# Expert outputs added by the scatter into four sums per token, in place of six rows

## What is computed

```
x = x + attn0(layernorm(x));  x = x + ffn0(layernorm(x))      # per-token attention; 2 experts, top 1
x = x + ssm(layernorm(x));    x = x + moe(layernorm(x))       # state space scan; 64 experts, top 6
def moe(h):                                                   # 2048 tokens, E = 64, TOP_K = 6, CAP = 64
    scores = softmax(h @ gate_w.T);  w, expert = top_k(scores, 6)
    for e in range(64):            # the first 64 (CAP) tokens that chose e, in token order; later ones are dropped
        out[e] = (silu(buf[e] @ w_gate[e]) * (buf[e] @ w_up[e])) @ w_down[e]
    y[t] = sum over the 6 choices of w[t, k] * out[expert[t, k]][slot of t]
    return y + shared expert(h)
```

## Time and profile before

| What | us |
|---|---|
| time, median of 3 runs | 720.53 |
| time of the profiled execution | 720.47 |
| its span in the profile | 718.7 |
| up to the first gather of an expert pair | 0 to 564.6 |
| pair stage, to the landing of the last scatter | 564.6 to 675.8 |
| loads, sums and stores of the result | 675.8 to 718.7 |

### The profile page before, as it was taken

One profiled execution on the slowest core, in us unless ns is written; L12 is line 12 of the kernel. 1 busy time (PEld: TensorE's weight loads), 2 busy tenths in 40 slices (PEclk: granted clock), 3 DMA queues, 4 the chain that ended last, 5 costly groups with the idle time before them and its releaser, 6 DMA issues.

```text
span 718.7 us, 7161 instructions
## 1 busy us (share of the span) xinstructions
PE 591.0 (82%) x2225; PEld 329.1 (46%) x2225; DVE 511.9 (71%) x1100; ACT 198.9 (28%) x387; POOL 105.6 (15%) x119
## 2 busy tenths in 40 slices
PE   4348999789999589988879997959658499999874
PEld 3234665436555445553444653543245144444553
DVE  4995878066986759998599996879965545555364
ACT  1111321225442064341633324412201133332100
POOL 3020221300002000002000020000000446664200
PEclk9766999998999699999998998979977699999999
DMA  8921000409101067011650023868071269998497
GB/s 312 382 86 45 29 31 9 124 31 351 67 29 36 1 236 249 1 37 29 236 212 1 1 66 119 293 229 289 0 241 38 64 242 371 363 358 299 148 412 295
DMA packets 50371, 114.35 MB, mean 159 GB/s; under 512 B 6112, under 2 KB 32992, under 8 KB 49824
## 3 DMA queue, kind: packets, MB, share of 16 engines
q1 hardware_dynamic: 42576, 94.88, 37.1%
q0 software_dynamic: 5456, 16.91, 6.9%
q10 hardware_dynamic: 2304, 2.10, 0.8%
HBM read 84.26 MB, written 29.62 MB: 158 GB/s over the span
## 4 chain that ended last, share of the span: by engine, by line
PE 52%; DVE 25%; DMA 6%; ACT 4%; issue 3%; SPq 2%; POOL 1%; DVEq 0%; POOLq 0%; ACTq 0%
PE gate_ps L675 7%; PE up_ps L675 7%; PE gate_ps L806 6%; PE misc_ps L692 6%; DVE scan_area L1219 6%; PE ssm_ps L725 4%; PE turn_ps L626 4%; DMA bc<-part_rows 3%; DVE scan_area L1215 3%; PE misc_ps L777 3%; PE ssm_ps L824 3%; DVE scan_area L1222 3%; PE misc_ps L824 2%; DVE sig L1159 2%; PE turn_ps L797 2%
## 5 line engine op out<-in xcount | busy, mean ns | idle before, releaser
L675 PE MATMUL gate_ps<-big,front_area 128*128 x160 | 81.1, 632 | 1.9 <-ACT front_area L864 1.9
L692 PE MATMUL misc_ps<-big,front_area 128*128 x320 | 75.1, 389 | 2.6 <-ACT front_area L864 1.6
L1219 DVE TENSOR_TENSOR_SCAN scan_area<-scan_area 128x1024 f32<-128x1024 f32 x32 | 73.3, 2292 | 5.5 <-ACT scan_area L964 2.0
L675 PE MATMUL up_ps<-big,front_area 128*128 x160 | 75.2, 592 | 0.0
L692 PEld LDWEIGHTS misc_ps<-big,front_area 128*128 128x128 f32 x320 | 62.0, 195 | 21.0 <-issue 13.1
L725 PE MATMUL ssm_ps<-scan_area,ident 128*128 128x512 f32 x128 | 62.8, 627 | 4.7 <-DVE scan_area L1222 4.2
L900 ACT ACTIVATE sig<-gate_ps 128x512 f32<-128x512 f32 (+1 forms) x52 | 30.9, 595 | 126.0 <-PE up_ps L675 90.0
L1159 DVE SCALAR_TENSOR_TENSOR sig<-sig,gate_ps 128x512 f32<-128x512 f32 (+1 forms) x52 | 35.5, 683 | 25.2 <-ACT sig L900 24.8
L964 ACT ACTIVATE scan_area<-scan_area,a_col 128x511 f32<-128x511 f32 x64 | 41.9, 713 | 32.0 <-DVE scan_area L1219 30.8
L584 POOL DMA_INDIRECT front_area<-ysorted_dram,slot_idx x16 | 18.0, 1126 | 220.6 <-DMA ysorted_dram<-front_area 217.0
L675 PEld LDWEIGHTS up_ps<-big,front_area 128*128 128x128 f32 x160 | 30.8, 192 | 39.6 <-issue 39.6
(11 more groups left out here) (213 smaller groups left out, 886.8 us busy)
## 6 DMA issues: line engine op xcount, KB each, us to landing
bc<-bc_dram SPq DMA_DIRECT2D x4, 4096.0 KB, 13.3
part_rows<-zeros SPq DMA_DIRECT2D x16, 768.0 KB, 16.4
big<-in_wgu SPq DMA_DIRECT2D x15, 704.0 KB
front_area<-in_wgu SPq DMA_DIRECT2D x9, 704.0 KB
big<-part_rows SPq DMA_DIRECT2D x8, 768.0 KB, 10.1
scan_area<-in_wgu SPq DMA_DIRECT2D x6, 704.0 KB
big<-in_wd SPq DMA_DIRECT2D x15, 256.0 KB
front_area<-part_rows SPq DMA_DIRECT2D x5, 768.0 KB, 20.7
```

The source lines that it names most:

```text
L675: mm = pe.matmul(bank[:], xs_t[:, k, j, :], gu0[:, expert_of[b, j], k, g, half * 512:(half + 1) * 512], start=(k == 0), stop=(k == K - 1))
L692: mm = pe.matmul(misc_ps[:, 0:D], h0_t[:, half, c * P:(c + 1) * P], dn0[:, expert_of[b, j], half * 4 + c, :], start=(half == 0 and c == 0) ...
L1219: nc.vector.tensor_tensor_scan(buf.rearrange(flat), d_a[:, g % 2, :, :].rearrange(flat), buf.rearrange(flat), 0.0, ALU.mult, ALU.add).then ...
```

## The change

`part_rows` now has four rows for each token, and the scatter adds to them instead of writing. The row is 4 x token + 2 x (pair number mod 2) + (which expert of the pair). So the rows that one scatter touches are all different, and so are those of neighbouring pairs, but pairs p and p-2 may add to the same row. GpSimd therefore waits before scatter p until scatter p-2 has landed. The rank of a choice is no longer needed.

```diff
 def places (DVE)
-                ts(chosen[:], marked[:, :, 0:E], -3.0, None, ALU.is_equal).then_inc(s, 1)
-                nc.vector.tensor_tensor_scan(nth[:].rearrange("p j e -> p (j e)"), flat, flat, 0.0, ALU.add, ALU.max
-                                             ).then_inc(s, 1)
-                stt(out=nth[:], in0=nth[:], scalar=-1.0, in1=wide(tok_value[:, bass.ds(b * J, J)], E),
-                    op0=ALU.mult, op1=ALU.add).then_inc(s, 1)
-                tt(placed.rearrange("p (q h e) -> p h q e", q=2, h=2), nth.rearrange(by_half, h=2),
-                   chosen[:].rearrange(by_half, h=2), ALU.mult).then_inc(s, 1)
+                for h in range(2):
+                    stt(out=by_half[:, h, :, :], in0=marked[:, 2 * h:2 * h + 2, 0:E], scalar=-3.0,
+                        in1=wide(tok_value[:, bass.ds(b * J + 2 * h, 2)], E), op0=ALU.is_equal, op1=ALU.mult).then_inc(s, 1)
 def tables (DVE); sum_no holds 2 * (pair mod 2) + expert of the pair
-                    nc.vector.tensor_copy(idx_put[rows, :], by_pair[rows, :, e]).then_inc(ids_steps, 1)
+                    stt(out=idx_put[rows, :], in0=by_pair[rows, :, e], scalar=SUMS / PER_TOKEN, in1=sum_no[rows, :],
+                        op0=ALU.mult, op1=ALU.add).then_inc(ids_steps, 1)
-                ts(idx_get, idx_put, 3, None, ALU.logical_shift_right).then_inc(ids_steps, 1)
+                ts(idx_get, idx_put, 2, None, ALU.logical_shift_right).then_inc(ids_steps, 1)
 GpSimd, at the start
-            pool.dma_start(empty_rows, zeros[:].unsqueeze(1).broadcast_to(empty_rows.shape)
+            pool.dma_start(table[N:TABLE_ROWS, :], zeros[0:CAP, :]).then_inc(scratch_clear, 16)
+            pool.dma_start(part_rows[SUMS * N:PART_ROWS, :].rearrange("(r p) d -> p r d", p=P),
+                           zeros[:, 0:D].unsqueeze(1).broadcast_to([P, SUMS * CAP // P, D])
                            ).then_inc(scratch_clear, 16)
+            pool.wait_ge(scratch_clear, 32)
 GpSimd, pair stage
             for p in range(PAIRS):
                 pool.wait_ge(yo_halves, 2 * (p + 1))
+                if p >= 2:
+                    pool.wait_ge(rows_put[(p - 2) % YO_RING], 16 * ((p - 2) // YO_RING + 1))
                 pool.indirect_dma_start(part_rows, bass.IndirectOffsetOnAxis(idx_put[:, p:p + 1], 0),
-                                        yo[:, p % YO_RING, :], None).then_inc(rows_put[p % YO_RING], 16)
+                                        yo[:, p % YO_RING, :], None, compute_op=ALU.add
+                                        ).then_inc(rows_put[p % YO_RING], 16)
                 if p + ROW_RING < PAIRS:
                     fetch(p + ROW_RING)
 SyncE clears and loads SUMS = 4 rows for each token in place of TOPK = 6; PE sums them
-                for k in range(TOPK):
+                for k in range(SUMS):
                     mm = pe.matmul(sum_ps[i], ident[:], parts[i][:, k * D:(k + 1) * D],
 DVE sums
                 tt(part[:, 0:half], part[:, 0:half], part[:, half:2 * half], ALU.add).then_inc(part_steps, 1)
-                tt(part[:, 0:D], part[:, 0:D], part[:, D:2 * D], ALU.add).then_inc(part_steps, 1)
-                tt(xt, xt, part[:, 2 * D:3 * D], ALU.add).then_inc(part_steps, 1)
-                tt(xt, xt, part[:, 0:D], ALU.add).then_inc(out_ready, 1)
+                tt(xt, xt, part[:, 0:D], ALU.add).then_inc(part_steps, 1)
+                tt(xt, xt, part[:, D:2 * D], ALU.add).then_inc(out_ready, 1)
```

More of the change, by code:

```diff
@@ L55 @@
 XW = D + E
-EMPTY = E * CAP
 PER_TOKEN = 8
-TABLE_ROWS = N + EMPTY // PER_TOKEN
-PART_ROWS = PER_TOKEN * N + EMPTY
+SUMS = 4
+TABLE_ROWS = N + CAP
+PART_ROWS = SUMS * TABLE_ROWS
 YO_RING = 4
@@ L75 @@
 GT = 4
-TOP = 2 * J + 6
+TOP = 2 * J + 4
 ROUNDS = CAP // 8
@@ L140, in build @@
         g0_row = sb("g0_row", [P, 2, D])
+        sum_no = g0_row[:, 0, 0:PAIRS]
         big = sb("big", [P, 2 * K * 2 * FF + 2 * 8 * D])
@@ L229, in build @@
         marked = sb("marked", [P, J, E + 2])
-        placed = marked[:].rearrange("p j e -> p (j e)")[:, 0:J * E]
-        chosen = sc
-        nth = att_s[:].rearrange("p r n -> p (r n)")[:, 0:J * E].rearrange("p (j e) -> p j e", j=J)
+        placed = sc[:].rearrange("p j e -> p (j e)")
         work = sb("work", [P, CAP + 2 * P])
@@ L257, in build @@
         yo = carve(YO_RING * D).rearrange("p (s d) -> p s d", s=YO_RING)
-        part_size = TOPK * D
+        part_size = SUMS * D
         parts = [mem[:, n * part_size:(n + 1) * part_size] for mem, count in ((big, 8), (front_area, 5), (area, 3))
@@ L277, in build @@
         part_rows = nc.dram_tensor("part_rows", (PART_ROWS, D), F32).ap()
-        part_of = part_rows[0:PER_TOKEN * N, :].rearrange("(i p r) d -> i p (r d)", p=P, r=PER_TOKEN)[:, :, D:D + part_size]
+        part_of = part_rows[0:SUMS * N, :].rearrange("(i p r) d -> i p (r d)", p=P, r=SUMS)
         x_loaded = [sem(f"x_loaded{b}") for b in range(B)]
@@ L504, in ssm_exp @@
                 for j in range(J):
-                    sp.dma_start(part_of[b * J + j].rearrange("p (r d) -> p r d", r=TOPK),
-                                 zeros[:, 0:D].unsqueeze(1).broadcast_to([P, TOPK, D])).then_inc(parts_clear, 16)
+                    sp.dma_start(part_of[b * J + j].rearrange("p (r d) -> p r d", r=SUMS),
+                                 zeros[:, 0:D].unsqueeze(1).broadcast_to([P, SUMS, D])).then_inc(parts_clear, 16)
             def weights(p):
@@ L559, in _ @@
                                              (last_slot[:], [[-P, J]], SLOTS - 1, -1),
-                                             (tok_value[:], [[-PER_TOKEN * L, B], [TOPK - PER_TOKEN * P, J]],
+                                             (tok_value[:], [[-PER_TOKEN * L, B], [-PER_TOKEN * P, J]],
                                               PER_TOKEN * N, -PER_TOKEN),
                                              (tile_thr[:], [[-P, S0]], L, 0),
-                                             (slot_no[:], [[1, CAP]], 0, CAP)):
+                                             (slot_no[:], [[PER_TOKEN, CAP]], 0, 0)):
                 nc.gpsimd.iota(dst, pattern, base=base, channel_multiplier=mult,
@@ L849, in _ @@
                     pe.wait_ge(last_added, 2)
-                for k in range(TOPK):
+                for k in range(SUMS):
                     mm = pe.matmul(sum_ps[i], ident[:], parts[i][:, k * D:(k + 1) * D],
-                                   start=(k == 0), stop=(k == TOPK - 1))
+                                   start=(k == 0), stop=(k == SUMS - 1))
                 mm.then_inc(parts_summed, 1)
@@ L1187, in ssm_proj @@
                     ts(a_col[:], a_col[:], -1.0, None, ALU.mult).then_inc(a_ready, 1)
+                    by_parity = sum_no.rearrange("p (n a) -> p n a", a=2)
+                    for e in range(2):
+                        for a in range(2):
+                            nc.vector.memset(by_parity[e * CAP:(e + 1) * CAP, :, a:a + 1], float(2 * a + e)
+                                             ).then_inc(dve_consts, 1)
             def ssm_delta(b, _):
@@ L1268, in places @@
                 dve.wait_ge(s, b * TOP + 2 * J + 2)
[L1269 to L1280 removed]
+                by_half = placed.rearrange("p (q h e) -> p h q e", q=2, h=2)
+                for h in range(2):
+                    stt(out=by_half[:, h, :, :], in0=marked[:, 2 * h:2 * h + 2, 0:E], scalar=-3.0,
+                        in1=wide(tok_value[:, bass.ds(b * J + 2 * h, 2)], E), op0=ALU.is_equal, op1=ALU.mult).then_inc(s, 1)
             values_turned = {}
@@ L1326, in tables @@
                 dve.wait_ge(turn_moved, turn.so_far())
+                dve.wait_ge(dve_consts, 10)
                 by_pair = ids_t.rearrange("p (n e) -> p n e", e=2)
@@ L1377, in _ @@
                 tt(part[:, 0:half], part[:, 0:half], part[:, half:2 * half], ALU.add).then_inc(part_steps, 1)
-                dve.wait_ge(part_steps, 3 * (i // 2) + 1)
-                tt(part[:, 0:D], part[:, 0:D], part[:, D:2 * D], ALU.add).then_inc(part_steps, 1)
-                tt(xt, xt, part[:, 2 * D:3 * D], ALU.add).then_inc(part_steps, 1)
-                dve.wait_ge(part_steps, 3 * (i // 2) + 3)
-                tt(xt, xt, part[:, 0:D], ALU.add).then_inc(out_ready, 1)
+                dve.wait_ge(part_steps, 2 * (i // 2) + 1)
+                tt(xt, xt, part[:, 0:D], ALU.add).then_inc(part_steps, 1)
+                dve.wait_ge(part_steps, 2 * (i // 2) + 2)
+                tt(xt, xt, part[:, D:2 * D], ALU.add).then_inc(out_ready, 1)
                 dve.wait_ge(parts_summed, i // 2 + 1)
```

1 line of the change is left out of this document (removed).

## The result

The changed kernel takes 729.29 us in the median (12 runs, 724.02 to 733.31), the kernel before 721.62 us beside it (12 runs, 719.08 to 725.67). The ratio is 1.009, with a 95% interval from 1.0065 to 1.0115. The forecast was 712.5 us, with a range to 727: the sign was wrong, and the range missed.

A forecast was written before the change was run, and what follows sets the result against it. Bounds taken: the TensorE and VectorE chain, then TensorE's pace with full DMA queues, then loads. 718.7 - 2.8 (choices) + 5.5 (adding and wait) - 10.0 - 0.7 (last part) = 710.7 us span, 712.5 us as measured; range 706.5 to 727.

The forecast's parts named there:

- What bounds the kernel: Chain of TensorE and VectorE until 564.6 us, then TensorE's pace with full DMA engines, then loads from 675.8 us.
- If it needs L, the scatters come L/2 apart ... Bounds for L: 2.8 ... to 10; I take 7.0: Pair stage, wait for scatter p-2: a landing of 7.0 us puts scatters 3.5 us apart instead of 3.08.
- The wait takes all: Second rival, pair stage: L of 8 or more; 722 us at 8, 726 to 727 at 8.5, 731 at 9; chance 0.24.
- the forecast's main case: Whole kernel: L from 6.2 to 7.6 and one more transfer pass give 710 to 718 us; chance 0.47.
- The rival's own argument against itself: Pair stage: against a long L, the idle landing of 2.38 us and a slower stage emptying the queues, shortening L.
- 25 x 0.385 = 9.6 us: Pair stage: some 25 adding scatters before the weights' end each cost one more pass of DMA time, 0.385 us.
- What queues behind the wait on GpSimd is the gather for pair p+8, 24 us ahead of its use, so no matter: Pair stage, GpSimd's queue: the gather held up behind the wait was priced at nothing.
- The slow read of the target: Pair stage: reading the target adds a memory wait of up to 2 us, 722 us in all; chance 0.08.
- Places, 2.8 us: Before the first gather: simpler choices save 1.34 us in `places.1`, 1.34 in `places.2`, 0.15 in `places.3`, together 2.8.
- places.3: Choices of the last batch: two instructions of 0.29 us replace four; only 0.15 us comes through, the rest becomes waiting.
- The last part, 10.7 us: After the last scatter: 4.19 MB fewer loads at 418 GB/s save 10.0 us, shorter VectorE work behind them 0.7.
- 4 us and more apart with TensorE below full busy (the wait): Sign in the profile after, pair stage: scatter spacing that would show the forecast wrong through the wait.

The follow-up runs named there:

- wait only: Kernel before with a wait for scatter p-2 and plain scatters: 727.99 us, ratio 1.0162.
- all that eases: Changed kernel with eight output buffers, gate and up loads split in four, and the gather issued ahead of the wait: 722.34 us, ratio 0.9999.
- the shorter rows: Changed kernel with gate and up loads split in four, rows of 1408 bytes instead of 5632: 726.48 us, ratio 1.0044.
- the eight buffers: Changed kernel with eight output buffers instead of four, so that `weigh` waits for p-8: 727.74 us, ratio 1.0075.
- the adding alone: Kernel before with the scatter made an adding one, no wait: 723.63 us, ratio 1.0056.
- empty queues: Changed kernel without the loads of the weights of pairs 12 to 31: 708.6 us, ratio 0.9795.
- plain scatters in four sums: Changed kernel with scatters that write instead of adding, the wait for p-2 kept: 717.63 us, ratio 0.9938.
- six sums: Changed kernel with six sums per token by pair number modulo 3, and a wait for p-3 instead of p-2: 721.66 us, ratio 0.9992.
- the one of before with both edits: Kernel before with adding scatters and the wait for scatter p-2: 743.62 us, ratio 1.0286.
- three cost 0 to 4: Kernel before with adding scatters and a wait for scatter p-3: 728.0 us, ratio 1.0057.

## Why the prediction was wrong, step by step

- **What bounds the kernel: right.** TensorE's pace, full transfer queues behind it and a last part bound by loads are what the experiments moved. That the queues were full was in the earlier trace rows. What I made too little of is that full queues are not only a price in bandwidth but lengthen every landing.
- **The failed step: "If it needs L, the scatters come L/2 apart ... Bounds for L: 2.8 ... to 10; I take 7.0".** The mechanism was named and a range given, but the number was too small in two ways. The landing is 8.0 us (the mean of six in the chain, 6.98 to 8.82), and the next scatter starts 0.77 us behind it, which the step left out. So two scatters take 8.9 us instead of 7.0. Put into the rival's own sum ("The wait takes all"), 8.9 gives 729 (redone, the sum gives 729.6 at 9, not 731); 729.3 was measured. It was given 0.24. That the two agree so closely is partly luck: the sum has the weights in at 668.7, and the DMA share of the change falls to 0.34 at 659; it counts 2.8 us for the choices, of which the profile shows 0.1, and 10.7 for a last part that gave 12.8. The argument for 7.0 was the store of the result, 7.2 in the median; but a plain scatter in the pair stage already lands in 6.5 to 7.0 (wait only), and the adding brings some 1.3 more in full queues, about what it brings in empty ones (3.8 against 2.4).
- **The right size for this step would not have been enough.** The kernel with all that eases has two scatters in 7.5 us, inside the 6.2 to 7.6 for which the forecast's main case gave 710 to 718. The forecast's own sum gives 717 for it, and 722.3 was measured. Some 2.2 of the 5 us are the choices, since its first gather starts 0.6 us earlier than before and not 2.8; the rest isn't traced, and the comparison is rough, since that kernel has the shorter rows and the eight buffers too.
- **The rival's own argument against itself failed.** I held against it that a slower stage empties the queues, which shortens L again. This came too late and was too little: while TensorE idles the DMA share stays 1.05 to 1.10 until 655. The backlog does shrink (from 640 on a pair's loads are issued as TensorE frees their place, at 640.45, 643.53, 647.21 and 650.61, and the last, issued at 651.9, is in by about 659, 7 us later, where the last with the adding alone took 19.6), and yet the gather at 647.12 still took 8.17 us to land.
- **"25 x 0.385 = 9.6 us"** of transfer time was mis-sized: with the adding alone the last weights land 5.0 us later, not 9.6. The Trainium skill, page "Collectives: The Full Stack", section "The bandwidth ceiling: the fold count and why AG ≠ RS ≠ AR", says of a reduce-scatter between cores that its additions read two sources and so halve the rate. The trace here fits that by one measure and not by the other: the packets of GpSimd's queue took 64.2 us (8.9% of 721.8) against 49.6 (6.9% of 718.7), 0.46 us more for each scatter, which is a pass more and above; but the loads beside them were delayed by only 0.2 us per scatter, half of the 0.385. In the changed kernel the term didn't matter at all, since the stage itself was slower than the loads.
- **"What queues behind the wait on GpSimd is the gather for pair p+8, 24 us ahead of its use, so no matter": wrong.** It stands in the change's chain at 647.12 with 8.17 us, and TensorE takes its rows up as it lands; with eight buffers it is in the chain twice. Eight pairs of lead are worth their time only while GpSimd's queue moves; a scatter that lags takes the gather behind it with it.
- **The slow read of the target** (a third of the second rival's chance): the adding costs 1.4 us of landing in empty queues (3.8 against 2.4), which is of the size of that rival's "up to 2 us". That it is the memory's read and not something else in the adding isn't shown.
- **Places, 2.8 us**: not seen in the profile of the change, where the first gather starts 0.1 us earlier. `places.3` does what was said (two instructions, 0.49 us). The start of the first gather differs from kernel to kernel by more than this (562.2 with plain scatters in four sums and 565.3 with six sums, both with the new choosing), so one execution can't tell. Over all the profiles of the table, the median is 563.3 with the new choosing (seven kernels) and 564.6 with the old (six): 1.3 us, half of the forecast, and the kernels with the same choosing differ by more than that.
- **The last part, 10.7 us**: right in kind, 12.8 in the profile. I divided the saved bytes by 418 GB/s, but that counts the result's stores too; the loads alone came at 1.57 MB per 4.4 us, 358 GB/s, which gives 11.7 for 4.19 MB. Places and last part together, 13.5 us as forecast, are 14.3 by the medians of the changed kernel and the one of before with both edits.
- **What would have been shown**: of the signs I named for "wrong", the one seen was "4 us and more apart with TensorE below full busy (the wait)".

What stays open: why the kernel with the wait alone and the one with four plain sums each lost some us around 665 in their profiles, in waits of ScalarE (4.05 and 6.85 us) whose releaser isn't shown; and what of a landing in full queues is the wait for other rows, since shorter rows took off only 0.5 of 8.0 us, and the memory may be what is waited for.

## What to carry to other kernels

Before a wait for a DMA's landing is put into a stage, measure the landing of that very transfer in that very stage, add the restart of the engine that waits, and divide by how many may be in flight: here 8.0 + 0.77 us needs a distance of three pairs at 3.1 us, and two cost 20 us (743.6 against 723.6) where three cost 0 to 4. A small transfer that something waits for is priced in full queues by its landing and not by its bytes, and the idle landing (3.8 us) is less than half of the full one. On an engine that serves its queue in order, a wait that is added also delays what stands behind it; issuing that first was a part of what made the last kernel even, though it wasn't tried alone.

## What the runs showed of the hardware

- An adding scatter of 128 rows of 1 KB takes 1.58 us of GpSimd's time against 0.99 for a plain one, and lands in 3.8 us against 2.4 with empty queues; in full queues 7.0 to 8.8 in the change (up to 9.9 in the kernel before with both) against 6.4 to 7.0.
- The Trainium skill, page "DMA: Bandwidth & Descriptors", section "Anatomy of one DMA — SWDGE (gpsimd) path", gives a fixed 2.0 us and bytes / 436 GB/s for a DMA, an estimate of 2.3 us for 128 KB. The trace agrees for the last plain scatter (2.38), and in full queues it is nearly three times that.
- From the landing to the start of the next scatter are 0.77 us in the change and 0.27 where the gather is issued ahead of the wait. Why it differs isn't shown.
- The DMA share rises with adding while the GB/s fall. A stretch of the kernel before, to be read beside that of adding alone:

```profile
600.00:620.00 20.00, 20.00 (x132) 8.13 (x131) 10.52 (x26) 6.67 (x21) 12.90 (x14) 1.00 1.03 366
```

1.03 and 366 GB/s became 1.08 and 348, and with empty queues the share is 0.54 at 92 GB/s. A share above 1 can't be room that is taken up once, and the adding scatters raise it by more than they take from the others: 0.46 us each in the packets of their queue, 0.2 us each in the landing of the last weights.
